# A transformer block on one core: norm rows of the first MLP groups in the last regular slots, up products in four banks, modulation on VectorE, last group in halves

## What is computed

```python
x_norm = modulate(_ln(x), shift_a, scale_a)           # c_proj = silu(c) @ W_mod + b_mod gives the six
x = x + gate_a * (self_attention(x_norm) @ W_proj + b_proj)
x = x + cross_attention(_ln(x), _ln(context)) @ W_cproj + b_cproj
x_norm2 = _ln(x) * (1 + scale_m) + shift_m
h = gelu_tanh(x_norm2 @ W_mlp1 + b_mlp1) @ W_mlp2 + b_mlp2
return x + gate_m * h
```

## Time and profile before

| what | us |
|---|---|
| runs (3) | 391.41, 389.43, 388.42; median 389.43 |
| profiled execution, its time | 390.49 |
| its span, first to last instruction | 388.7 |
| busy in the span: PE / DVE / ACT / POOL | 341.4 / 259.0 / 272.2 / 211.1 |

### The profile page before, as it was taken

The page is one execution under the profiler, slowest core; times in us unless marked ns, Lnnn a source line. Parts: engine busy times, 40 slices in busy tenths (PEclk is TensorE's granted clock), DMA queues, the critical chain, the costliest instruction groups (busy, mean ns, idle before and its releaser), DMA issues. The chain is left out here.

```text
span 388.7 us, 15992 instructions
## 1 busy us (share of the span) xinstructions
PE 341.4 (88%) x5880; PEld 230.6 (59%) x5880; DVE 259.0 (67%) x658; ACT 272.2 (70%) x533; POOL 211.1 (54%) x478
## 2 busy tenths in 40 slices
PE   3767877889898999999999999998987698899994
PEld 2545544566676767777677677775654345454442
DVE  5764648767788789798888888877845524443401
ACT  1246464778788888888888879887776747576672
POOL 7862667767576686777867777766355100112100
PEclk9998889999999999999999999999999989999998
DMA  5354264544344443444434444344131100101001
GB/s 159 88 129 116 58 154 100 143 114 112 89 100 112 96 108 85 96 110 97 110 84 97 109 101 113 77 116 99 44 87 36 49 3 3 29 27 54 27 27 54
DMA packets 65548, 33.13 MB, mean 85 GB/s; under 512 B 8359, under 2 KB 65255, under 8 KB 65511
## 3 DMA queue, kind: packets, MB, share of 16 engines
q1 hardware_dynamic: 63183, 32.29, 34.0%
q10 hardware_dynamic: 2328, 0.33, 0.6%
HBM read 4.83 MB, written 2.10 MB: 18 GB/s over the span
## 5 line engine op out<-in xcount | busy, mean ns | idle before, releaser
L815 DVE TENSOR_REDUCE mx<-wide 128x8 f32<-128x1024 f32 x64 | 78.2, 1221 | 29.0 <-PE wide L1277 28.7
L1014 ACT ACTIVATE p_c<-wide 128x1024 f32<-128x1024 f32 x64 | 65.6, 1025 | 26.6 <-PE wide L1288 25.6
L1014 ACT ACTIVATE p_s<-wide 128x1024 f32<-128x1024 f32 x64 | 65.7, 1027 | 12.3 <-PE wide L1288 12.0
L815 DVE TENSOR_REDUCE mxc<-wide 128x8 f32<-128x616 f32 x64 | 50.8, 794 | 9.8 <-PE wide L1277 9.6
L1299 PE MATMUL ps_o<-p_s,v_m 128*32 128x128 f32 x1024 | 42.4, 284 | 0.2
L1299 PE MATMUL ps_o<-p_c,vc_m 128*32 128x128 f32 x1024 | 41.7, 281 | 0.3 <-ACT p_c L1014 0.3
L1277 PE MATMUL wide<-qk_st 62*128 62x128 bf16 x512 | 26.6, 226 | 11.2 <-DVE mx L815 6.6
L1277 PEld LDWEIGHTS wide<-qk_st 62*128 62x128 bf16 x512 | 15.2, 97 | 27.2 <-DVE mx L815 14.7
L1340 PE MATMUL wide<-m_nT,w_sb 128*128 128x512 f32 x64 | 29.7, 599 | 0.2 <-DVE mxc L815 0.2
L1299 PEld LDWEIGHTS ps_o<-p_s,v_m 128*32 128x32 f32 x1024 | 25.0, 111 | 7.5 <-issue 1.9
L1299 PEld LDWEIGHTS ps_o<-p_c,vc_m 128*32 128x32 f32 x1024 | 24.3, 110 | 7.3 <-ACT p_c L1014 0.8
(11 more groups left out here) (163 smaller groups left out, 824.7 us busy)
## 6 DMA issues: line engine op xcount, KB each, us to landing
qkc_st<-qkcp SPq DMA_DIRECT2D x96, 128.0 KB, 2.5
qk_st<-qkp SPq DMA_DIRECT2D x94, 128.0 KB, 2.5
out<-m_out SPq DMA_DIRECT2D x8, 256.0 KB, 2.3
xs<-x SPq DMA_DIRECT2D x3, 512.0 KB, 4.0
qk_st<-nmT SPq DMA_DIRECT2D x64, 4.0 KB
qkc_st<-nmcT SPq DMA_DIRECT2D x64, 4.0 KB
ctx_sb<-ctx SPq DMA_DIRECT2D x3, 308.0 KB
w_sb<-L_xcond_W_mlp SPq DMA_DIRECT2D x2, 256.0 KB, 4.3
```

The costliest lines, as they stand in the source:

```text
L815: nc.vector.reduce_max(mxt[:, b].rearrange("q (x r) -> q r x", r=2)[:, r], src, AX.X, negate=True).then_inc(sems[done], 1)
L1014: nc.scalar.activation(dst[u % 2][:].rearrange("k x q -> k (x q)"), ps_st[:].rearrange("k s x -> k (s x)"), ACT.Exp, scale=SCALE).then_inc ...
```

## The change

Group 0's and group 1's norm rows are made in slots 14 and 15: VectorE's statistics at the head of beat 0, the scaling at the head of beat 5, GpSimd's step ahead of the slot's first split of the maxima. Group 0 is transposed at the head of the tail, group 1 and 2 earlier than before; all transposes use `ps_misc[2]`. VectorE modulates groups 0, 1 and 2. Group 0's up products use all four halves of `wide`, the free ones first. In the tail VectorE takes group 2's statistics and scaling before p13's residual. The last group's down products, gates, transposes, sums and store are made in two halves of 256 columns (2 batches) each. The diff, cut to its core:

```diff
+    def group(self):
+        return self.k if isinstance(self.i, int) and self.i == NPAIR // 2 - 1 else None
...
-            return wide[0 if isinstance(g, int) and g == 0 else k // 2][:, k % 2]
+            return wide[1 - k // 2 if isinstance(g, int) and g == 0 else k // 2][:, k % 2]
...  SP
-            with sp.Fori(0, NGRP // 2) as i:
+            with sp.Fori(0, NGRP // 2 - 1) as i:
                 store(2 * i, 0)
                 store(2 * i + 1, 1)
+            store(NGRP - 2, 0)
+            for n in range(2):
+                lo = B - MG + 2 * n
+                w(sp, "m_out_set", NGRP + n)
+                sp.dma_start(out[lo:lo + 2].rearrange("b t c -> t b c"),
+                             m_out[1][:, 2 * n:2 * n + 2]).then_inc(sems["out1"], 16)
...  POOL, slot
+                if s.group() is not None:
+                    m_rstd_step(s.group())
                 if h:
                     split_max(h, 0, mx, nm, "mx_set", "nmh_set", "nm_set", "mts_ps")
...  DVE, slot: m_norm is cut into m_moments (stats, aggr) and m_normalise (wait for rstd, scaling)
+                    if t == 0 and s.group() is not None:
+                        w(dve, "x2_set", 2 * s.group() + 2)
+                        m_moments(s.group())
+                    if t == 5 and s.group() is not None:
+                        m_normalise(s.group(), s.group())
...  DVE, tail
             residual(p12, "projc_ps", "proj_c", "x2_set")
-            w(dve, "x2_set", 2)
-            m_norm(0, 0, True)
+            m_modulate(0, 0)
             attention_out(p15, "s", "o_t", "ot_ps", "rden_set", "o_set", "obt_ps")
...
             cross_maxima(p14, [3])
+            w(dve, "x2_set", 6)
+            m_moments(2)
+            m_modulate(1, 1)
+            m_normalise(2, 0)
             residual(p13, "projc_ps", "proj_c", "x2_set")
-            m_norm(1, 1)
             cross_maxima(p15, range(NU))
             cross_out(p14)
             m_gate(0, 0)
-            m_modulate(1, 1)
             residual(p14, "projc_ps", "proj_c", "x2_set")
+            m_modulate(2, 0)
             cross_out(p15)
-            m_norm(2, 0)
+            m_norm(3, 1)
             residual(p15, "projc_ps", "proj_c", "x2_set")
             m_residual(0, 0, True)
-            m_norm(3, 1)
             m_residual(1, 1, True)
...  ACT: m_modulate(0, 0) and m_modulate(2, 0) taken out; group 0's GELU 1 ahead of p14's second row copy
-            m_gelu(0, 0, [0])
+            m_gelu(0, 0, [1])
             cross_max_rows(p14, 1)
...  PE, tail
             self_values(p15, 2)
+            after("x1_t", p14, 2)
+            m_transpose(0, 0, True)
...
             max_scores(s16, (p14, 2), "cross")
             project(after("x1_t", p15, 2), p15, wdh[:, 2], x1T[:], "x1T_set", "qc_ps")
+            flip_sums(after("o_t", p15, 1), "c", p13, "sumc_set", "oct_ps")
...
             max_scores(s16, (p14, 3), "cross")
+            m_up(0, 0, True, [0, 1])
             flip_out(after("oc_t", p13, 1), "c", p13, "oc_set", "obct_ps")
+            after("q_c", p15, 2)
+            m_transpose(1, 1, True)
+            m_up(0, 0, True, [2])
             max_t(after("max_c0", p14, 0), p14, 1, nmc, "nmc_set", "mtc_ps")
+            m_up(0, 0, True, [3])
             cross_proj(after("obc_t", p13, 1), p13)
-            m_up(0, 0, True, [2, 3])
...
+            exp_scores(s17, (p14, 2), "cross")
             max_t(after("max_c1", p14, 0), p15, 0, nmc, "nmc_set", "mtc_ps")
-            exp_scores(s17, (p14, 2), "cross")
...
             cross_values(p15, 1)
-            m_transpose(1, 1, True)
+            m_up(1, 1, chunks=[0])
...
+            m_transpose(2, 0)
             cross_values(p15, 3)
-            m_up(1, 1, chunks=range(2))
+            m_up(1, 1, chunks=[1])
+            m_up(1, 1, chunks=[2, 3])
             flip_sums(after("proj_c", p14, 1), "c", p15, "sumc_set", "oct_ps")
...
             m_back(0, 0, True)
-            m_transpose(2, 0)
+            flip_out(after("oc_t", p15, 1), "c", p15, "oc_set", "obct_ps")
+            m_down(1, 1, True)
             cross_proj(after("obc_t", p15, 1), p15)
-            m_down(1, 1, True)
...  PE, end (ACT's gates and DVE's sums wait for their half likewise)
-            m_down(NGRP - 1, 1)
-            m_back(NGRP - 1, 1)
+            w(pe, "m_hT_set", NF * NGRP)
+            for n in range(2):
+                for k in range(NF):
+                    last = mm((ps_misc[1], ps_o)[n][:, 0:GT], w2_sb[:, k], hT[1][:, k, n * GT:(n + 1) * GT],
+                              start=(k == 0), stop=(k == NF - 1))
+                last.then_inc(sems["m_y_ps"], 1)
...
```

More of the change, by code:

```diff
@@ L841, in one, with m_moments @@
                 return xs[:, at].rearrange("t o c -> t (o c)")
-            def m_norm(g, par, first=False):
-                if not first:
+            def m_moments(g):
+                if not (isinstance(g, int) and g == 0):
                     hold(dve, "m_n_set", g)
@@ L852, in m_norm, with m_normalise @@
                 last.then_inc(sems["m_mv_set"], 1)
-                if not first and not (isinstance(g, int) and g < 2):
+            def m_normalise(g, par):
+                if not (isinstance(g, int) and g < 2):
                     hold(dve, "m_nt_ps", g - 1)
@@ L859, in m_norm @@
                 last.then_inc(sems["m_n_set"], 1)
+            def m_norm(g, par):
+                m_moments(g)
+                m_normalise(g, par)
             def m_residual(g, par, first=False):
@@ L1217, in _ @@
             cross_max_rows(p14, 0)
+            m_gelu(0, 0, [0])
             cross_rows(p13)
-            m_gelu(0, 0, [0])
+            m_gelu(0, 0, [1])
             cross_max_rows(p14, 1)
-            m_gelu(0, 0, range(1, NF))
+            m_gelu(0, 0, range(2, NF))
             cross_exps(p14, [0, 1])
@@ L1244, in _ @@
             m_gelu(NGRP - 1, 1)
-            m_gate(NGRP - 1, 1)
+            for b in range(MG):
+                w(act, "m_y_ps", NGRP + b // 2)
+                nc.scalar.activation(m_y[1][:, b * T:(b + 1) * T],
+                                     (ps_misc[1] if b < 2 else ps_o)[:, b % 2 * T:(b % 2 + 1) * T], ACT.Identity,
+                                     bias=one(gb_m, NGRP - 1, b), scale=one(mod[:, 5], NGRP - 1, b)
+                                     ).then_inc(sems["m_y_set"], 1)
         @block.tensor
@@ L1335, in m_up @@
                 for k in chunks:
-                    if first and k >= 2:
-                        w(pe, "m_hT_set", k - 1)
-                    elif not first:
+                    if first:
+                        w(pe, *(("expc_set", NU * (NPAIR - 2)) if k < 2 else ("mxc_set", NU * (NPAIR - 1))))
+                    else:
                         w(pe, "m_hT_set", NF * g - NF + k + 1)
@@ L1580, in _ @@
             exp_scores(s16, (p13, 2), "cross")
-            flip_out(after("x1_t", p14, 2), "s", p15, "o_set", "obt_ps")
+            w(pe, "m_nT_set", 1)
+            flip_out(ps_misc[2], "s", p15, "o_set", "obt_ps")
             cross_values(p13, 1)
             self_proj(after("ob_t", p15, 2), p15)
-            after("o_t", p15, 1)
-            m_transpose(0, 0, True)
             exp_scores(s16, (p13, 3), "cross")
@@ L1613, in _ @@
             max_scores(s17, (p15, 2), "cross")
+            exp_scores(s17, (p14, 2), "cross")
             max_t(after("max_c1", p14, 0), p15, 0, nmc, "nmc_set", "mtc_ps")
-            exp_scores(s17, (p14, 2), "cross")
             cross_values(p14, 1)
-            after("q_c", p15, 2)
+            w(pe, "m_nT_set", 2)
             m_down(0, 0, True, [0])
@@ L1639, in _ @@
             cross_proj(after("obc_t", p14, 1), p14)
+            w(pe, "m_y_set", 1)
+            m_transpose(2, 0)
             cross_values(p15, 3)
-            m_up(1, 1, chunks=range(2))
+            m_up(1, 1, chunks=[1])
+            w(pe, "expc_set", NU * NPAIR)
+            m_up(1, 1, chunks=[2, 3])
             flip_sums(after("proj_c", p14, 1), "c", p15, "sumc_set", "oct_ps")
-            w(pe, "expc_set", NU * NPAIR)
-            m_up(1, 1, chunks=range(2, NF))
-            flip_out(after("oc_t", p15, 1), "c", p15, "oc_set", "obct_ps")
             after("max_c1", p15, 0)
             m_back(0, 0, True)
-            m_transpose(2, 0)
+            flip_out(after("oc_t", p15, 1), "c", p15, "oc_set", "obct_ps")
+            m_down(1, 1, True)
             cross_proj(after("obc_t", p15, 1), p15)
-            m_down(1, 1, True)
             with pe.Fori(1, NGRP // 2 - 1) as i:
@@ L1662, in _ @@
             m_back(NGRP - 2, 0)
-            m_down(NGRP - 1, 1)
-            m_back(NGRP - 1, 1)
+            w(pe, "m_y_set", NGRP - 1)
+            w(pe, "m_hT_set", NF * NGRP)
+            for n in range(2):
+                for k in range(NF):
+                    last = mm((ps_misc[1], ps_o)[n][:, 0:GT], w2_sb[:, k], hT[1][:, k, n * GT:(n + 1) * GT],
+                              start=(k == 0), stop=(k == NF - 1))
+                last.then_inc(sems["m_y_ps"], 1)
```

(6 more changed lines are left out.)

34 lines of the change are left out of this document (15 added, 19 removed).

## The result

The changed kernel takes 383.87 us (median of 4 runs, 383.08 to 385.17) against 389.59 (4 runs, 388.42 to 391.41): ratio 0.985, 95% interval 0.981 to 0.990. Forecast 384.4; as a difference, 5.7 us against the forecast 5.0. The profiled execution took 383.61, its span is 381.6.

The account below looks back on a forecast made before the run. TensorE was taken to bound the regular slots and MLP loop; only the stretch between them and the end could give time back. +3.3 - 6.9 - 1.4 = -5.0 from 389.43 gave 384.4 us, range 381.2 to 388.0.

Parts of the forecast that it names:

- Part 2: Tail up to group 0's last GELU: earlier up products in four banks end that GELU 2.0 us earlier.
- Part 4: Tail up to the MLP loop: waits gone, chiefly 2.43 us for group 2's norm; gain 2.8 us.
- Part 5: Last group in halves: fewer gates left at the end and a halved last store; gain 1.4 us.
- the term -1.0: Slot 15's start: the existing 0.97 us DMA wait for p15's stack swallows 1.0 us of the slots' delay.
- Part 3: p14's and p15's cross attention: earlier reductions and a full clock, so scores come 4.1 us earlier, the GELU's gain included.
- Part 1: Norm rows of groups 0 and 1 in slots 14 and 15: VectorE's added work costs 3.3 us.
- GpSimd at nothing: Slots 14 and 15: GpSimd's step of 1.01 us costs nothing, as the split behind it waits for VectorE anyway.
- Not limited by SP: Tail, p14's rows: issued at 301.5 us, they land about 2.3 later, before the exponential can start.
- I expect it not to fall: Tail's cross attention: TensorE's clock stays up, as only some 1.5 us of standing remain; saves 1.5 us.
- Rival (b): The clock falls again in the tail, so its 1.5 us stay: 385.9 us; chance 0.18.
- The stand: Before the MLP loop: new TensorE wait of 0.6 us behind p15's sums, for VectorE's two instructions.
- 0.4 of idle bits: Before the MLP loop: group 1's first up chunk fills two idle bits around the exponentials, gaining 0.4 us.

Follow-up runs that it names:

- e5: Changed kernel with group 0's up products in the two halves of wide[0] again; 0.989 of the kernel before.
- e6: Changed kernel with groups 0 and 2 modulated by ScalarE instead of VectorE; 0.989 of the kernel before.
- e3: Changed kernel with the last group whole again instead of in halves; 0.982 of the kernel before.
- e7: Changed kernel with the scaling of groups 0 and 1 moved from beat 5 to the end of slots 14 and 15; 0.983 of the kernel before.
- e8: As e7, with the statistics at beat 2 and GpSimd's step behind the slot's key and query parts; 0.976 of the kernel before.
- e9: Changed kernel timed once more without edits; 383.62 us, 0.984 of the kernel before.
- e10: e8 timed once more without edits; 382.50 us, 0.982 of the kernel before.
- e4: Changed kernel with the norm of groups 0 and 1 left out, raw rows transposed instead; 0.974 of the kernel before.
- e11: As e8, with p15's sums transposed one up chunk earlier and the last group's wait for its fourth GELU covered; 380.92 us, 0.976 of the kernel before.
- e2: Kernel before with only the last group in halves; 0.995 of the kernel before.
- e1: Kernel before plus the norm work of groups 0 and 1 in slots 14 and 15, into unread buffers; 1.006 of the kernel before.

## Why the prediction was right, and where it was not

The median came within 0.5 us of the forecast. The two traces, laid side by side, differ by 6.2 us and not by 5.0: the slots cost less than forecast and part 2 gained more, parts 4 and 5 gained less. In each part the places that cost or gain are the ones named. Two terms came out by luck: the -1.0 for the DMA in the slots, and the clock in part 3.

- **Part 1, slots: over-sized.** 3.3 forecast, 2.4 between the two traces. The places were right, all of them; each term was too large. Slot 14's statistics: the second scores came 1.80 after the first before, 2.45 in the changed kernel, so 0.65 for 0.9. What is left of slot 14's +0.63, with the 0.97 of the DMA taken in, is 0.95 for the scaling, forecast 1.2. In slot 15 the same two are 0.71 for 1.0 and, as the rest of +1.76, 1.05 for 1.2. "GpSimd at nothing" held.
- **Part 1, the term -1.0: luck.** The wait of 0.97 went, but not for the reason given. I had the parts of the stack late by 0.9 only. Counted from slot 14's first scores, its last issue began at 14.51 instead of 12.92, so 1.59 later, 0.65 from GpSimd's parts and the rest from SP's queue, which took 1.58 us for one issue before it instead of 0.62. The landing then took 2.43 us instead of 3.64. With 3.64, by this estimate, it would have been late by 0.8 again (14.51 + 3.64 against 17.32), and slot 14 as much longer. e5, with the same slots, paid 1.50.
- **Part 2: under-sized.** 2.4 with the 0.4 of the first transpose, measured 3.19. Two terms: p15's query came 1.2 earlier instead of 1.0 (from p13's first cross scores, 11.2 for 12.4), and four GELUs with two copies took 2.93 instead of 3.4, since each starts before the one ahead of it has ended. About 0.1 is left open. That four banks carry it is shown by e5 (2.34); that group 0's modulation is better off ScalarE by e6 (1.4, at e6's place). "Not limited by SP" was wrong by 0.34, the wait for p15's stack.
- **Part 3: right, by luck in part.** -2.1 forecast, -2.17 measured in the first profile. It holds 1.5 for a clock that I expected to stay up. In the profiles of e3, e6, e7, e8, e9 and e10 it fell once in the tail, in those of the changed kernel, e4, e5 and e11 not: "I expect it not to fall" is the step that failed, though it did not show in the first profile. Rival (b), to which I gave 0.18, happened in six of these ten. The ground that I gave against it, that the idle gaps are smaller now, did not carry: in e9 no wait of TensorE in the 4.5 us before the fall was longer than 0.67. The old tail pays the clock too, in all three of its profiles (before, once at 310.7; e2, for 6.8 us; e1, three times), so part of the gain remains, but how often each kernel pays was not measured.
- **Part 4:** -2.8 forecast, -2.32 measured. The stand was 0.63 (forecast 0.6), the 2.43 went, and group 1's transpose (0.6). These three make 2.4. The 0.4 of idle bits was not there to be had: the trace of the kernel before has one wait of 0.20 around the exponentials, and so has the changed kernel's.
- **Part 5:** -1.4 forecast, 1.12 here and 1.22 in e2 and e3. The start waited 0.43 instead of 0.3; the rows already say so, as the last GELU ended at 379.67 and the old down products began at 379.21. The second gates took 0.80 as forecast, and each transpose and sum one hand-over more. From the last down product's end to the span's end it is 4.0 us (forecast 4.1, before 5.9).
- **The spans and the medians.** The difference of the spans is 7.1, of which 1.0 lies ahead of the change; the medians differ by 5.7.

## What to carry to other kernels

Work moved ahead into a stage that the other engine bounds is paid for at every wait that it lengthens, however idle the engine that does it looks; put it right before a wait that is there anyway, and do not count a wait for a DMA that one trace shows as room, before other executions show it too. Undo a change part by part and compare stretches between events that both traces have: in the tail they repeat to 0.01 us as long as the clock stays, where the times scatter by 3. A stretch with a DMA on its path does not repeat, and wants several traces. And in an order written by hand, look behind each transposition for the other engine's two instructions, and put a chunk of products there.

## What the runs showed of the hardware

- TensorE's clock in the same program at the same place is at the 1.2 GHz level in one execution and at 2.4 in the next (e9 and the first profile of the changed kernel), and in both TensorE had worked in the same way before (2.06 and 2.05 us busy of 3.2). One such stretch of 3.4 us cost between 0.96 (e7) and 1.58 us (e10). The Trainium skill (TensorE: Matmul & The Clock Gate, What you observe) says that the moment of the transition to the full clock varies from run to run. Here it varies whether the clock falls at all, which that section does not speak of.
- The last part of p15's stack, issued from SP's queue with the same instructions, landed 2.4 to 4.3 us after its issue and let TensorE wait 0 to 1.77 us. In all twelve profiles that record it, the late landings (3.6 or more, seven) have a 16 KB load of instructions that began at most 1.4 us behind the issue, and the early ones (2.5 or less, five) have it 1.9 us behind or later. The load itself took 0.9 to 1.7 us. The packets that started only behind it make it the likely cause; no run tried it.
- A store of 128 KB landed in 1.8 us, one of 256 KB in 2.3.
